# A four-layer kernel's first cross attention: its key pass rewritten, with rotation halves in separate blocks, 32-row score tiles and the next layer's keys projected there

## The reference, cut to what matters

```python
def _L0_xattn_ref(x, latents, ...):        # x is ctx_1024 (12544 tokens), latents the 128 queries
    xn = layer_norm(x, gamma_x, beta_x)
    ln = layer_norm(latents, gamma_l, beta_l)
    q = (ln @ Wq).reshape(b, m, h, d)      # h = 8, d = 64
    kv_x = xn @ Wkv
    k_x = rope_rotate_k(k_x)               # k * cos + [-k[half:], k[:half]] * sin, half = 32
    ...                                    # latents' own keys and values are joined on
    # softmax over all keys of q.k * d ** -0.5, times v, then Wo

def _L1_xattn_ref(q, k, v, mask, wq, bq, wk, bk, wv, bv):
    kp = k @ wk.T + bk                     # k is ctx_1024, not normalized
    ...
```

## Time and profile before

| | us |
|---|---|
| median of 3 runs | 2975.75 (2972.16 to 2976.79) |
| the profiled execution's own time | 2981.08 |
| its span in the profile | 2979.3 |
| TensorE busy over the span | 2414.8 (81%) |
| VectorE busy | 1906.6 (64%) |
| ScalarE busy | 1273.8 (43%) |
| GpSimd busy | 455.4 (15%) |

### The profile page before, as it was taken

The page is one execution under the profiler, slowest core; times in us unless marked ns, Lnnn a source line. Parts: engine busy times, 40 slices in busy tenths (PEclk is TensorE's granted clock), DMA queues, the critical chain, the costliest instruction groups (busy, mean ns, idle before and its releaser), DMA issues. The chain is left out here.

```text
span 2979.3 us, 58562 instructions
## 1 busy us (share of the span) xinstructions
PE 2414.8 (81%) x21882; PEld 1496.0 (50%) x21882; DVE 1906.6 (64%) x3107; ACT 1273.8 (43%) x2039; POOL 455.4 (15%) x260
## 2 busy tenths in 40 slices
PE   3488869999997483999995779999995336999978
PEld 3333335555554381666663645655555232555547
DVE  7589976776766615666653148778884837777721
ACT  2177763333333323777774213233330132555552
POOL 0044430000000000000000005566551200000000
PEclk8599989999999795999997789999997567999989
DMA  7445463455551164667661523222221143776726
GB/s 237 163 161 185 175 198 115 136 144 145 146 154 66 34 245 122 158 156 163 160 141 24 185 81 117 100 86 86 86 98 36 42 100 88 155 163 147 157 63 228
DMA packets 240547, 390.69 MB, mean 131 GB/s; under 512 B 31425, under 2 KB 201767, under 8 KB 240267
## 3 DMA queue, kind: packets, MB, share of 16 engines
q1 hardware_dynamic: 240394, 388.47, 45.3%
HBM read 310.42 MB, written 78.01 MB: 130 GB/s over the span
## 5 line engine op out<-in xcount | busy, mean ns | idle before, releaser
L2422 PE MATMUL l2x_kf<-l2x_w,l2x_nin 128*128 128x512 f32 x784 | 341.6, 596 | 6.8 <-DMA l2x_nin<-scratch_nT 6.8
L1611 DVE CUSTOM_DVE_ANT_0 l1x_junk<-l1x_pm,l1x_mrow,l1x_top 128x896 bf16<-128x896 f32 x224 | 247.1, 1149 | 108.2 <-PE l1x_pm L1750 105.6
L1611 DVE CUSTOM_DVE_ANT_0 l3x_junk<-l3x_pm,l3x_mrow,l3x_top 128x896 bf16<-128x896 f32 x224 | 246.0, 1148 | 89.2 <-PE l3x_pm L1750 88.8
L1679 ACT ACTIVATE l1x_prob<-l1x_ring,l1x_mask_col 128x512 f32<-128x512 f32 x392 | 248.2, 684 | 114.4 <-PE l1x_ring L1770 113.1
L1682 ACT ACTIVATE l3x_prob<-l3x_ring 128x512 f32<-128x512 f32 x392 | 213.0, 594 | 161.6 <-PE l3x_ring L1774 161.6
L1397 POOL TENSOR_TENSOR l2x_side_rest<-l2x_side_xin,l2x_side_kp 128x1792 f32<-128x1792 f32 x14 | 50.3, 3595 | 1339.2 <-ACT l2x_side_kp L1373 1339.2
L2422 PEld LDWEIGHTS l2x_kf<-l2x_w,l2x_nin 128*128 128x128 f32 x784 | 148.6, 191 | 191.4 <-issue 188.9
L2404 ACT ACTIVATE l2x_fsq<-l2x_f 128x1024 f32<-128x1024 f32 x98 | 103.6, 1057 | 286.8 <-DVE l2x_f L2369 286.8
L815 PE MATMUL l0x_max_pk<-l0x_max_xin,l0x_wk 128*128 128x448 f32 x448 | 199.0, 570 | 29.1 <-PE l0x_max_ps L836 14.4
L2468 POOL TENSOR_TENSOR l2x_gk<-l2x_f,l2x_ks 128x1024 f32<-128x1024 f32 x98 | 182.3, 1896 | 159.9 <-DVEq L2394 159.9
L1202 PE MATMUL l0x_att_pv<-l0x_wv,l0x_att_vin 128*128 128x512 f32 x392 | 194.4, 619 | 1.3 <-DVE l0x_att_tops L1083 1.3
(11 more groups left out here) (688 smaller groups left out, 4768.2 us busy)
## 6 DMA issues: line engine op xcount, KB each, us to landing
l1x_kt<-scratch_KS SPq DMA_DIRECT2D x84, 448.0 KB, 9.1
l3x_kt<-scratch_KS SPq DMA_DIRECT2D x84, 448.0 KB, 9.3
scratch_KT<-l0x_max_kf SPq DMA_DIRECT2D x28, 896.0 KB, 5.5
l0x_att_kt<-scratch_KT SPq DMA_DIRECT2D x56, 448.0 KB, 7.5
scratch_KS<-l0x_side_kp SPq DMA_DIRECT2D x14, 1344.0 KB, 13.3
scratch_KS<-l2x_side_kp SPq DMA_DIRECT2D x14, 1344.0 KB, 6.0
l0f_w<-L_ffn_exp_w SPq DMA_DIRECT2D x16, 1024.0 KB, 7.0
l1f_w<-L_ffn_W SPq DMA_DIRECT2D x16, 1024.0 KB, 6.3
```

Source lines behind the costliest of these rows:

```text
L1611: dve.tensor_tensor_reduce(junk[x % 2][:, :, :], pm[x % 2][:, :, 0:SPLIT], mrow[b][:, :].rearrange("p (s k) -> p s k", s=2), 1.0, top[1 - ...
L1679: ins = act.activation(into, scores, ACT.Exp, bias=R.mask_col[:, bass.ds(m * TILES + n // 4, 1)])
L2422: last = pe.matmul(pf[u][:, n, :], nin[b][:, c, t * P:(t + 1) * P], w[:, c, n * BANK:(n + 1) * BANK], start=(c == 0), stop=(c == DC - 1))
```

## The change

`rotated_keys` takes the place of `find_maximum`, and `attend` loses the projection of the second layer's keys.

- The columns of the key and query weights are put in another order (`halves_together`), so that blocks 0 and 1 hold the first rotation halves of heads 0 to 3 and 4 to 7 (32 rows a head), and blocks 2 and 3 the second halves. The two operands of a rotation now lie in the same rows of two blocks, `pa` and `pb`, and nothing is exchanged.
- VectorE makes four products for each pair of blocks (L597 to L605), eight in a chunk, all from PSUM; GpSimd makes the difference and the sum, four operations of 448 in a chunk.
- The scores are sums of two matmuls over 32 rows, 16 in a chunk, four heads in four row groups of the array and four PSUM banks `ps` (L713). ScalarE copies them to SBUF as bf16, 896 elements at a time, four in a chunk (L657), and VectorE folds each half (128x1792, bf16) into a running maximum (L611). The reduction to `top` is made once, behind the last chunk.
- The raw context is loaded in the key pass too, TensorE projects the second layer's keys there (`other_keys`, two blocks of 128 rows a chunk, through the single bank `p1`), ScalarE copies them out (L643), and they are stored as `scratch_K1`. In the attention pass `side` loads these, and its four projections and four copies a chunk are gone.

```diff
@@ rotated_keys, vector and scalar
+                def rotate(b, i, p):
...
+                    after(dve, sem("b_proj"), n + 1)
+                    half = bias_k[:, 2 + p:3 + p]
+                    dve.scalar_tensor_tensor(terms[p][:, 1, :], pb[:, 0:MAX_CHUNK], half, cs[b][:, 1, :],
+                                             ALU.add, ALU.mult)
...
+                def fold(b, i, p):
+                    after(dve, sem(f"copied{p}"), 2 * number(b, i) + 2)
+                    after(dve, sem(f"folded{p}"), number(b, i) + 1)
+                    dve.tensor_tensor(running[p][:, :, :], running[p][:, :, :], near[p][:, :, :], ALU.max).then_inc(
+                        sem(f"folded{p}"), 1)
...
+                def both(ahead, now):
+                    rotate(*ahead, 0)
+                    fold(*now, 0)
+                    rotate(*ahead, 1)
+                    fold(*now, 1)
...
+                def other_keys(b, i, c):
...
+                    after(act, sem("k1_proj"), DC * number(b, i) + c + 1)
+                    act.activation(k1[b][:, c, :], p1[:, 0:MAX_CHUNK], ACT.Identity,
+                                   bias=bias1[:, c:c + 1]).then_inc(sem("k1_read"), 1)
...
+                def copy_scores(b, i, p):
+                    after(act, sem(f"scored{b}"), 2 * i + p + 1)
+                    after(act, sem(f"folded{p}"), number(b, i) + 1)
+                    for h in range(0, HEADS, 2):
+                        act.activation(near[p][:, h:h + 2, :], psc[:, h:h + 2, 0:MAX_CHUNK], ACT.Copy).then_inc(
+                            sem(f"copied{p}"), 1)
...
+                def both(ahead, now):
+                    copy_scores(*now, 0)
+                    copy_scores(*now, 1)
+                    other_keys(*ahead, 0)
+                    round_keys(*ahead, 0)
+                    other_keys(*ahead, 1)
+                    round_keys(*ahead, 1)
@@ rotated_keys, tensor
+                def other_keys(b, i, c):
...
+                    after(pe, sem("k1_read"), DC * number(b, i) + c)
+                    project(p1, w1, b, slice(c * P, (c + 1) * P), raw).then_inc(sem("k1_proj"), 1)
+                    if c == DC - 1:
+                        after(pe, sem("k1_proj"), DC * number(b, i) + DC)
...
+                def scores(b, i, p):
+                    after(pe, sem(f"kb{b}"), 2 * i + p + 1)
+                    after(pe, sem(f"copied{1 - p}"), 2 * number(b, i) + 2 * p)
+                    for ab in range(2):
+                        for hh in range(HEADS):
+                            rows = slice(32 * hh, 32 * hh + 32)
+                            last = pe.matmul(psc[:, hh, 0:MAX_CHUNK], qb[rows, 2 * ab + p, :], kb[b][rows, 2 * ab + p, :],
+                                             start=(ab == 0), stop=(ab == 1))
...
+                def both(ahead, now):
+                    block_of_keys(*ahead, 0)
+                    scores(*now, 0)
+                    other_keys(*ahead, 0)
+                    block_of_keys(*ahead, 1)
+                    scores(*now, 1)
+                    other_keys(*ahead, 1)
@@ attend
-                        if 1 <= s < 5:
-                            side.evacuate(act, m, s - 1)
                         if s in (2, 4):
                             side.high(act, m, s // 2 - 1)
...
-                        if t % TILES < 4:
-                            side.project(pe, 2 * i + t // TILES, t % TILES)
```

More of the change, by code:

```diff
@@ L574, in spill @@
-                def spill(b, i):
[L575 to L583, removed]
+                    n = bass.ds(number(b, i), 1)
@@ L602, in _ @@
-                ahead = min(steps - 1, 2)
-                if steps - 1 > ahead:
-                    with sp.Fori(0, steps - 1 - ahead) as i:
-                        load_and_spill(i)
-                else:
-                    for i in range(0, steps - 1 - ahead + 1):
-                        load_and_spill(i)
-                    ahead -= 1
+                        load_next(b, i)
+                        spill(b, i)
                 for b in range(2):
@@ L864, in _, with project @@
-                if masks == "key":
-                    pe.wait_ge(S.sem("mask_in"), 16)
-                if project:
-                    run_ahead(pe, steps, project_all, project_and_score, score_all)
-                else:
-                    with pe.Fori(0, steps) as i:
-                        score_all(0, i)
-                        score_all(1, i)
+                def project(out, w, b, cols, x):
+                    for d in range(DC):
+                        last = pe.matmul(out[:, 0:MAX_CHUNK], w[:, d, cols], x[b][:, d, :], start=(d == 0),
+                                         stop=(d == DC - 1))
+                    return last
@@ new lines, in prepare @@
+                def prepare(b, i):
+                    for p in range(2):
+                        block_of_keys(b, i, p)
+                        other_keys(b, i, p)
+                def both(ahead, now):
[5 more added lines that the diff above has]
+                    other_keys(*ahead, 1)
+                def score_all(b, i):
+                    scores(b, i, 0)
+                    scores(b, i, 1)
@@ L2154, in _ @@
                     pe.wait_ge(S.sem("klb"), 1)
-                    for h in range(H):
-                        last = pe.matmul((ps0 if h < 4 else ps1)[:, (h % 4) * P:(h % 4 + 1) * P],
-                                         qb[h // 2][:, h % 2, :], klb[:, h // 2, :], start=True, stop=True)
+                    for p in range(2):
+                        for ab in range(2):
+                            for hh in range(4):
+                                rows = slice(32 * hh, 32 * hh + 32)
+                                last = pe.matmul(lscores[hh][:, p * P:(p + 1) * P], qb[rows, 2 * ab + p, :],
+                                                 klb[rows, 2 * ab + p, :], start=(ab == 0), stop=(ab == 1))
                     last.then_inc(S.sem("latent_scores"), 1)
```

475 lines of the change are left out of this document (163 added, 312 removed).

## The result

The changed kernel takes 3035.9 us (median of 4 runs, 3031.56 to 3042.95), the kernel before 2975.36 (4 runs) on the same chip: ratio 1.0198, 95% interval 1.0184 to 1.0212. It is slower by 2.0%, at the predicted 3036. The profiled executions differ by less, 3035.41 against 2981.1, since the one of before lay 5 us above its median; the traces therefore have to account for 54.3 us of span (2979.3 to 3033.6).

The account below looks back on a forecast made before the run. VectorE was taken to bound the key pass and TensorE the attention pass. Terms -95 + 39 + 81 + 1 + 23 + 11 = +60 gave 3041 us from the profiled 2981.1, or 3036 from the median; range 2960 to 3090.

Parts of the forecast that it names:

- What goes, -95: Attention pass: 56 second-layer projection steps of 1.70 us leave TensorE, 95 us off; every tile then takes 4.03 us.
- What is late next, +39: Attention pass: TensorE waits 3.0 us at tile 3, its exponential queued behind a split awaiting a store; 13 chunks, +39.
- Clock in the attention pass, +11: Attention pass: half of 13 TensorE gaps lower the clock, at 1.7 us each, +11.
- Key pass, +80 for 27 chunks: Key pass: a chunk lasts 13.05 us instead of 10.08, TensorE's work 10.55 plus a 2.5 us wait for p1.
- Ends, stop and setup: Key pass: +3 before the loop, +3 behind it, -4.6 for a load stop that goes; setup +1.
- Clock in the key pass, +23: Key pass: half of the gaps in 27 chunks lower TensorE's clock, at 1.7 us each, +23.
- The clock after every gap (3070): Both passes: TensorE's clock falls after every gap, +94 in all, 3070 us; chance 0.12.
- The store in time: Attention pass: the store lands by T + 13, before TensorE needs tile 3; +10 in all, 2986 us; chance 0.14.
- The key pass at TensorE's own pace, 2946: Key pass: ScalarE isn't late with p1, so chunks take TensorE's 10.55 us; -30 in all, 2946 us; chance 0.12.
- 32-row matmuls one after another: Key pass: 32-row matmuls don't overlap as four, +2.3 us a chunk, +61, 3097 us; chance 0.08.

Follow-up runs that it names:

- two kp buffers: Changed kernel with a second buffer for the attention pass's split keys (kp), so a split needn't wait for the previous chunk's store: 2984.5 us, ratio 1.0012 to before.
- ScalarE's order: Changed kernel with ScalarE's first read of p1 in the key pass moved ahead of the second score copy: 2974.6 us, ratio 0.9981 to before.
- the fold left out: Changed kernel without VectorE's bf16 fold of each chunk's first four score rows, whose maxima don't enter the result: 3040.2 us.
- the folds behind both rotations: Kernel with layer two's keys projected in the attention pass again, plus VectorE doing both rotations before both folds: 2954.7 us, ratio 0.9914 to before.

## Why the prediction was right

**What goes, -95.** Tiles take 4.03 us. Putting the projections back costs 41 us of the attention pass, and without the wait that their going uncovered they are worth 513.5 - 417.9 = 96, where 95 was taken. Right.

**What is late next, +39.** 38.8 us in 12 stops of 3.2 us, where 13 of 3.0 were taken, by the split that starts at T + 16.6 where T + 16.2 was taken. Right; the two kp buffers show that the store alone does it.

**Clock in the attention pass, +11.** 15.8 us, as the two buffers took back 54.6 with 38.8 of stops. Nine of the 12 stops show low windows, not half of 13. Their length doesn't decide which: in TensorE's timeline the first of these two lost the clock (0.69 in the window from 830), the second didn't (1.00 from 860 to 870).

```profile
828.55 1.09 PE L1133 MATMUL l0x_O<-l0x_att_pt,l0x_att_v 128*64 128x128 f32 x16 [2.81 <-ACT l0x_att_pt L1039]
...
861.98 1.09 PE L1133 MATMUL l0x_O<-l0x_att_pt,l0x_att_v 128*64 128x128 f32 x16 [3.30 <-ACT l0x_att_pt L1039]
```

**Key pass, +80 for 27 chunks.** The gap, taken as 2.5, is 2.35, with its releaser as named; the edit of ScalarE's order gave back 62.8 of 27 x 2.35 = 63.5. The term that was mis-sized is TensorE's own work, taken as 10.55. Measured, from starts in the rows above, six projections take 1.77 + 3 x 1.60 + 1.61 + 1.50 = 9.68 instead of 9.4: the one ahead of TensorE's wait for its own end takes 1.77, those next to a burst or behind that wait 1.60 or 1.61, and only one 1.50; two bursts take 1.05 instead of 0.76 (the second stands ahead of the gap, with its tail); the wait for its own end is 0.6 on average instead of 0.39. That makes 11.33, +21 us over 27 chunks, and the shorter gap takes back 4: 13.68 against 13.05, 97 instead of 80. GpSimd's four adds were mis-sized too, 6.2 us a chunk instead of 4.6, but TensorE never waits for them, and ScalarE 3.0 us in the whole pass.

**Ends, stop and setup.** The pass grew by 96.3, of which chunks are 97; ends, stop and setup together gave -1, predicted +2. The stop is gone as said: the chunk behind the first load of the attention pass lasts 13.9.

**Clock in the key pass, +23.** This step failed in the profiled execution: from 155 to 525 us the clock is 1.00 in every window, though TensorE stops 2.35 us in each chunk. The same instructions lost it four times with two kp buffers and four times with the fold left out, and their key passes are 5.3 and 5.0 us longer. The term's size is 0 to 5, not 23. The Trainium skill (TensorE: Matmul & The Clock Gate, on HAM oscillation) tells of a kernel in which every wait for data between groups of matmuls let the clock fall, and puts that down to how long these waits were. That any short gap must pay, as the prediction read it, is more than it says, and the traces don't show it: neither at 2.35 nor at 3.19 us did every gap pay.

**The sum: luck in part.** In the traces the key pass with its setup grew by 96.3 us where 81 + 1 + 23 = 105 was forecast, and the attention pass shrank by 42.0 where 45 was. Within the key pass the shortfall of 23 in the clock and the excess of 17 in the chunk mostly cancel. The traces give +54.3, some 6 under the forecast of +60. That the medians lie 60.5 apart, and the forecast within 1 us, is luck: it was made for the profiled execution of before, which lay 5 us above its median, and the changed kernel's lay at its own.

**The rivals.** The clock after every gap (3070): refuted at this gap; with 0.85 us more on ScalarE most gaps pay, but still not each. The store in time: refuted, it lands at T + 16.6. The key pass at TensorE's own pace, 2946: refuted for the changed kernel, and the kernel with ScalarE's order is what it spoke of, and that takes 2974.6, 29 above 2946. 21 of these are the mis-sized work of TensorE (27 x 0.78), 6 the attention pass, 475.6 where 45 less than 514.5 was forecast; the rest is within the 3.1 us by which that chip is slower (2978.9 for before against 2975.75). 32-row matmuls one after another: refuted, eight in 0.49.

**What the prediction didn't say:** of the two parts of the change the remade maxima are worth 7 us alone (299.1 to 292.2), although VectorE's work by chunk fell from 9.0 us (35.85/40 x 10.08) to 7.6 (22.26/40 x 13.7). The move of K1 costs the key pass 104 us, 63 of them by ScalarE's order, and gives the attention pass 41, or 96 once the store is out of the way. With both waits gone the changed kernel is 60 us below before on the same chip, and 79 without the wait for its own end.

What stays open is when the clock falls. Gaps of 1.75 to 1.85 us in chunks of 9.25 lost it seven times, gaps of 2.35 in chunks of 13.7 never or four times, and a stop of 3.30 us kept it where one of 2.81 lost it, so the length alone doesn't decide. No run separates the causes.

## What to carry to other kernels

When work moves into a stage whose bound engine is being relieved, look at each in-order queue for a reader of a single bank that stands behind a copy which waits for later work: here two swapped lines are 61 us. When a stage gets shorter, look at which transfer was hidden behind it: a wait that costs nothing today (47.9 us on ScalarE) is the next stop of TensorE. A stop of TensorE can cost more than its length: at 3.2 and 4.0 us in each chunk the half clock put 1.6 and 1.9 us on top on average, at 2.35 us nothing or little. And TensorE's wait for its own end cost 0.27 us a chunk in the projections around it beside the 0.59 of idle time shown.

## What the runs showed of the hardware

VectorE's bf16 maximum of two tiles in SBUF and GpSimd's f32 add hold each other up. VectorE's timeline in the changed kernel, one fold:

```profile
304.84 1.17 DVE L611 TENSOR_TENSOR l0x_max_running<-l0x_max_running,l0x_max_near 128x1792 bf16<-128x1792 bf16 x1 [0.98 <-ACT l0x_max_near L657]
```

GpSimd's timeline, an add of the prologue, where no fold runs, and the one beside that fold:

```profile
153.27 1.13 POOL L751 TENSOR_TENSOR l0x_max_kf<-l0x_max_terms 128x448 f32<-128x448 f32 x1
...
305.02 1.98 POOL L751 TENSOR_TENSOR l0x_max_kf<-l0x_max_terms 128x448 f32<-128x448 f32 x1
```

The add takes 0.85 us longer beside the fold, and with the folds in a row VectorE itself loses 0.84 us (3.02 for two of 1.09). VectorE's products, which read PSUM, don't do this. In the kernel with the folds behind both rotations this one, on VectorE, lies across the end of one of GpSimd's operations and the start of the next:

```profile
308.31 0.68 DVE L592 SCALAR_TENSOR_TENSOR l0x_max_terms<-l0x_max_pb,l0x_bias_k,l0x_max_cs 128x448 f32<-128x448 f32 x1 [0.68 <-PE l0x_max_pb L676]
```

Both of GpSimd's stay at 1.14:

```profile
307.71 1.14 POOL L736 TENSOR_TENSOR l0x_max_kf<-l0x_max_terms 128x448 f32<-128x448 f32 x1 [1.46 <-DVE l0x_max_terms L600]
308.80 1.14 POOL L738 TENSOR_TENSOR l0x_max_kf<-l0x_max_terms 128x448 f32<-128x448 f32 x1
```

The Trainium skill (SBUF — State Buffer, Who interferes with whom) says that an instruction of VectorE with two inputs in SBUF contends with a GpSimd instruction that reads SBUF; these rows agree. That the waiting one stands still for just the other's length is not shown by them: the fold lasts until 306.01, the add began at 305.02 and lost 0.85 of that 0.99.
